# Layer 3's self-attention: rounded probabilities as low bytes of half-precision words, their base taken off by products

## The chip, the cores and the metric

The kernel runs on one core of a Trainium2 chip. The metric is the device time of one launch in microseconds (us). A profiled execution records every instruction with its start, its duration and the wait before it; its own time stands beside its span below. Engine names are those of the profile: PE is TensorE's matmul, PEld its weight load, DVE VectorE, ACT ScalarE, POOL GpSimd, SPq the queue of SyncE, from which the DMAs start.

## What is computed

Four small transformer layers follow each other on a state of 2 images x 512 tokens x 128 features, with a context of 2 x 77 x 128. The change concerns the self-attention of the fourth, layer 3, with 16 heads of 8 features. Queries, keys, probabilities and values are quantised to 8 bits there. Cut to this attention, the reference is:

```python
def _fq(x, delta, zp, n_bits):
    xi = _round_ste(x / delta) + zp
    xq = jnp.clip(xi, 0.0, 2.0 ** n_bits - 1.0)
    return (xq - zp) * delta
q, k, v = heads of h1 @ wq, h1 @ wk, h1 @ wv          # h1 = layer norm of x
sim  = einsum('bhid,bhjd->bhij', _fq(q, dq, 128.0, 8), _fq(k, dk, 128.0, 8)) * SCALE
attn = softmax(sim)
out  = einsum('bhij,bhjd->bhid', _fq(attn, dw, 0.0, 8), _fq(v, dv, 128.0, 8))
x = out @ wo + bo + x
```

So each probability becomes an integer from 0 to 255, each value an integer from -128 to 127, and their products are summed over 512 keys for every head and query.

## The kernel before, in words

Each engine has its own program (`block.sync`, `block.gpsimd`, `block.tensor`, `block.scalar`, `block.vector`), and semaphores tie them together. The self-attention of layer 3 is a pipeline over PAIRS = 64 pairs of heads: 2 images (b) x 4 values of v x 4 blocks of 128 queries (qb) x 2 pairs (`pair_of`). The 128 partitions of a tile are 4 bands of 32, and a pair is two neighbouring bands, j = 0 and 1; head 4 * band + v lies in a band at features 8 v to 8 v + 7. For pair n:

- PE (`int_scores`, L1339) makes the scores of both bands, 2 x 128 queries x 512 keys, in PSUM banks 2 (n % 3) and the next. It waits until the exponentials of pair n-3 have left these banks.
- DVE (`maxima`, L2197) reduces them to a negated maximum per query and head. POOL (`shift`, L565) multiplies it by the scale. ACT (L1644) takes two exponentials of 512 columns with their sums into a ring of six tiles (`e_ring`, parts of `e_buf` and `t_buf`); each sum comes out of its accumulator by a short instruction of its own.
- Once for two pairs, DVE (`recips`, L2203 and L2204) multiplies four sums by the step and takes the reciprocals.
- POOL (`rounded`, L574) multiplies the exponentials by the reciprocal and writes them as int16, which rounds, into `t_rows`, two instructions of 128 x 512. This is done for pair n-3 (ROUND_BEHIND) after the shift of pair n.
- SP (L411) starts one DMA transpose per pair, 128 x 1024 two-byte words, from `t_rows` to `t_turned`, rings of TURNING = 5.
- DVE (`keys`, L2210) clamps the transposed integers at 255 and converts them to bf16 in `t_keys`, a ring of four, for pair n-7 (KEYS_BEHIND) behind the maxima of pair n.
- PE (`int_outputs`, L1359) multiplies them by the values in `v_band` for pair n-8 (VALUES_BEHIND) behind the scores of pair n: 8 products of 128 columns, one per block of keys and band, each with a weight of 128 x 32 into its band of bank 7. The values of one head stand in its 8 of 32 columns and the others are zero, so that all heads of a band add up in one bank. Four products with a zero weight (L1353) open the bank for each image.

The order of work on each engine is that of the program text: for every n PE does scores of n, outputs of n-8; DVE maxima of n, `prepare(n)` (values, second half of queries and keys, key masks, for n up to 12), reciprocals, keys of n-7; POOL shift of n, rounding of n-3; ACT the exponentials of n. At fixed n other work is woven in: at 40 the output projection of image 0 (L785 on PE, 8 products; `add_to_x` on DVE), statistics and normalisation at 41 to 47, at 44 a reciprocal square root on POOL (L482, L484), at 48 and 50 a transposition and the cross queries on PE, at 52 to 54 their conversion on DVE, at 60 to 64 dummy products on PE (`keep_warm`, L641), and from 66 the first scores of the cross-attention (`first`, L1067). POOL's program ahead of the stage ends with the normalisations of layer 2 and 3 (`rstds_of`, L482 and L484; `add_bias`, L496).

```python
for n in range(PAIRS + KEYS_BEHIND):        # DVE
    if n < PAIRS: maxima(n)
    prepare(n)
    m = n - ROUND_BEHIND
    if 0 <= m < PAIRS and m % 2 == 0: recips(m // 2)
    if n >= KEYS_BEHIND: keys(n - KEYS_BEHIND)
```

Of the kernel before, what the change touches and what calls it, by code (L numbers as in the profile page):

```python
# [9 lines left out]
I16 = mybir.dt.int16  # L10
ALU = mybir.AluOpType
# [3 lines left out]
P = 128  # L15
# [79 lines left out]
TURNING = 5  # L95
# [25 lines left out]
MAX_AT = 320  # L121

# [24 lines left out]
def build(nc, ins, out, stop=99):  # L147
    ctx = ExitStack()
    with ctx:
# [29 lines left out]
        def S(name):  # L179
# [101 lines left out]
        v_band = q_stack[:, 6 * NT:10 * NT].rearrange("p (t b h c) -> p t b h c", b=B, h=H, c=BAND)  # L281
        t_rows = [k_stack[:, i * NT:(i + 1) * NT].bitcast(I16).rearrange("p (j n) -> p j n", j=2) for i in range(TURNING)]
        t_turned = [k_stack[:, i * NT:(i + 1) * NT].bitcast(I16) for i in range(TURNING, 2 * TURNING)]
        t_keys = [k_stack[:, i * NT:(i + 1) * NT] for i in range(2 * TURNING, 2 * TURNING + 4)]
# [6 lines left out]
            for places in (((q_stack[:, 10 * NT:], 0), (q_stack[:, 10 * NT:], 1)),  # L291
                           ((q_stack[:, 10 * NT:], 2), (q_stack[:, 10 * NT:], 3), (k_stack[:, (2 * TURNING + 4) * NT:], 0)),
                           ((k_stack, 0), (k_stack, 1), (k_stack, 2))))
        flat_rows, flat_turned = ([a.bitcast(I16) for a in t] for t in (flat_rows, flat_turned))

# [5 lines left out]
        v_one = sb("v_one", [P, QB, B, H, VW])  # L301
        e_ring = [e_buf[:, i // 2, i % 2 * NT:(i % 2 + 1) * NT].rearrange("p (j n) -> p j n", j=2) for i in range(4)]
# [75 lines left out]
        def _(sp):  # L378
# [26 lines left out]
            if stop >= 3:  # L405
                for n in range(PAIRS):
                    done, value = turned(n)
                    sp.wait_ge(S("ints.rounded"), 2 * (n + 1))
                    if n >= TURNING:
                        sp.wait_ge(S("ints.pt"), n - TURNING + 1)  # L410
                    sp.dma_start_transpose(t_turned[n % TURNING].rearrange("p (c q) -> p c q", q=P),  # L411
                                           t_rows[n % TURNING].rearrange("p j n -> p (j n)")).then_inc(done, 16)
                for i in range(T):
                    done, value = turned(PAIRS + i)
                    sp.wait_ge(S("cross.rounded"), i + 1)
                    if i >= len(flat_turned):
                        sp.wait_ge(S("cross.keys"), i - len(flat_turned) + 1)
                    sp.dma_start_transpose(flat_turned[i % len(flat_turned)].rearrange("p (c q) -> p c q", q=P),
                                           flat_rows[i % len(flat_rows)]).then_inc(done, 16)
# [9 lines left out]
        def _(pool):  # L429
# [130 lines left out]
            def shift_pairs():  # L560

                def shift(n):
                    c = 2 * (n % 8)
                    pool.wait_ge(S("ints.nm"), n + 1)
                    pool.tensor_scalar(stats[:, 1, c:c + 2], stats[:, 0, c:c + 2], sders[:, 8:9], None, ALU.mult  # L565
                                       ).then_inc(S("ints.m"), 1)

                def rounded(n):
                    pool.wait_ge(S("ints.recip"), n // 2 + 1)
                    if n >= TURNING:  # L570
                        pool.wait_ge(*turned(n - TURNING))
                    for j in range(2):
                        c = 2 * (n % 8) + j
                        pool.tensor_scalar(t_rows[n % TURNING][:, j, :], e_ring[n % len(e_ring)][:, j, :],  # L574
                                          stats[:, 2, c:c + 1], 0.0, ALU.mult, ALU.add).then_inc(S("ints.rounded"), 1)

                for n in range(PAIRS + ROUND_BEHIND):
                    if n < PAIRS:
                        shift(n)
                    if n >= ROUND_BEHIND:  # L580
                        rounded(n - ROUND_BEHIND)
                    if n == RSTD_AT:
                        rstds_of("L3.ln2", 0)
# [14 lines left out]
            if stop >= 2:  # L598
# [9 lines left out]
                for h in range(B):  # L608
                    rstds_of("L2.ln3", h)
                    add_bias("L2.ff", "L2.ln3.xh", h, h + 1)  # L610
            if stop >= 3:
# [14 lines left out]
        def _(pe):  # L626
# [697 lines left out]
            if stop >= 3:  # L1324
# [18 lines left out]
                def int_outputs(n):  # L1343
                    pair, b, v, qb = pair_of(n)
                    pe.wait_ge(S("ints.pt"), n + 1)
# [5 lines left out]
                    if n % (PAIRS // B) == 0:  # L1351
                        for band in range(BANDS):
                            pe.matmul(ps[BAND * band:BAND * (band + 1), 7, :], no_weight[:, :], half(k_int, b),  # L1353
                                      start=True, stop=False)
                    for kb in range(QB):
                        for j in range(2):
# [3 lines left out]
                                           v_band[:, kb, b, V * band + v, :], t_keys[n % len(t_keys)][:, c:c + P],  # L1360
# [306 lines left out]
        def _(dve):  # L1667
# [462 lines left out]
            if stop >= 3:  # L2130
# [29 lines left out]
                def values(k):  # L2160
                    dve.wait_ge(S("L3.v.base"), 1)
                    for v in range(V):
                        ins = dve.tensor_scalar(
                            v_band[:, :, k, :, :].rearrange("p t (j v) c -> p t j v c", v=V)[:, :, :, v, DH * v:DH * (v + 1)],
                            gel[:, k, :].rearrange("p (t j v d) -> p t j v d", t=QB, j=BANDS, v=V)[:, :, :, v, :],
                            MAGIC, None, ALU.subtract)
                    ins.then_inc(S("L3.values"), 1)
# [38 lines left out]
                def keys(n):  # L2206
                    dve.wait_ge(*turned(n))
                    if n >= len(t_keys):
                        dve.wait_ge(S("ints.pv"), n - len(t_keys) + 1)
                    dve.tensor_scalar(t_keys[n % len(t_keys)], t_turned[n % TURNING], QMAX, None, ALU.min  # L2210
                                      ).then_inc(S("ints.pt"), 1)

                cross_maxima, cross_recips, rest = cross()
                for n in range(PAIRS + KEYS_BEHIND):
# [6 lines left out]
                    if n >= KEYS_BEHIND:  # L2221
                        keys(n - KEYS_BEHIND)
# [66 lines left out]
```

## Time and profile before

| | before |
|---|---|
| median of 3 runs | 520.34 us (519.62 to 522.51) |
| the profiled execution, its own time | 520.02 us |
| its span, first to last instruction | 518.2 us |
| mean granted clock of TensorE, share of 2.4 GHz | 0.864 |
| PE busy, share of the span | 414.1 us, 80% |
| DVE | 354.9 us, 68% |
| ACT | 254.6 us, 49% |
| POOL | 241.1 us, 47% |

The self-attention of layer 3 lies between about 306 and 444 us of the span. The busy shares are over the whole program; what an engine does in this stage is read from windows. Neighbouring instructions of one engine overlap a little in the records, so a group's busy time is somewhat above the time from its first start to the next group's start. The weight loads run beside the products.

### The profile page before, as it was taken

To read this page: it belongs to the slowest core of one execution; us is meant where nothing else is said; L and a number is where in the kernel's file an instruction comes from. 1 tells how busy PE (TensorE), PEld (TensorE's weight loads), DVE (VectorE), ACT (ScalarE), POOL (GpSimd) and SP (SyncE) were. 2 spreads that over 40 slices of the span, in tenths; PEclk is the share of its full clock that TensorE was granted. 3 is DMA by queue.
4 is the path that set the end of the run, shared out by engine and by line. 5 is a ranking of instruction groups with operands and counts; after the bars stand their busy time and mean duration, and the time that the engine had idled before them with its cause. 6 is when DMAs were issued, how large, how long until landed. Compare 5 with 4: busy or idle time off the path is not lost.

```text
span 518.2 us, 8441 instructions
## 1 busy us (share of the span) xinstructions
PE 414.1 (80%) x2920; PEld 206.7 (40%) x2932; DVE 354.9 (68%) x802; ACT 254.6 (49%) x513; POOL 241.1 (47%) x378
## 2 busy tenths in 40 slices
PE   5999878898888999998998753666655668977797
PEld 3647544544335334333345530222232223433536
DVE  1756764559999012266873489999989898689552
ACT  2224434232002667634354338899977784457441
POOL 5052234565000443525010326999978897236420
PEclk9899999999999999999999995555565655689999
DMA  9500000000000000000000004798876669113301
GB/s 254 180 1 3 3 2 0 1 0 1 2 1 0 1 1 2 1 1 1 0 2 1 1 1 58 147 151 152 145 123 122 116 133 159 28 25 76 77 0 42
DMA packets 88976, 26.11 MB, mean 50 GB/s; under 512 B 81061, under 2 KB 88167, under 8 KB 88935
## 3 DMA queue, kind: packets, MB, share of 16 engines
q1 hardware_dynamic: 88935, 25.58, 25.5%
q8 instruction: 24, 0.39, 0.3%
q14 instruction: 17, 0.14, 0.1%
HBM read 5.61 MB, written 0.52 MB: 12 GB/s over the span
## 4 chain that ended last, share of the span: by engine, by line
PE 40%; DVE 29%; POOL 20%; issue 6%; DMA 2%; ACT 2%; POOLq 0%; DVEq 0%; ACTq 0%
POOL k_stack L574 12%; DVE k_stack L2117 9%; PE ps L849 5%; PE ps L864 4%; POOL stats L565 3%; PE ps L751 3%; DVE stats L2197 3%; PE ps L644 3%; DVE xh L1688 3%; PE ps L761 2%; DVE st L1679 2%; PE ps L641 2%; POOL rstd L484 2%; PE ps L825 2%; PE ps L927 1%
## 5 line engine op out<-in xcount | busy, mean ns | idle before, releaser
L2197 DVE TENSOR_REDUCE stats<-ps 128x2 f32<-128x1024 f32 x64 | 77.7, 1214 | 2.4 <-PE ps L1339 2.1
L1644 ACT ACTIVATE e_buf<-ps,stats,sders 128x512 f32<-128x512 f32 x88 | 67.7, 774 | 18.4 <-POOL stats L565 18.4
L1359 PE MATMUL ps<-k_stack,q_stack 128*32 128x128 bf16 x512 | 37.7, 302 | 36.9 <-DVE k_stack L2210 36.9
L574 POOL TENSOR_SCALAR k_stack<-e_buf,stats 128x512 int16<-128x512 f32 x88 | 62.7, 723 | 2.1 <-DVE stats L2204 1.5
L1490 ACT ACTIVATE e_buf<-ps 128x1024 f32<-128x1024 f32 (+3 forms) x44 | 28.2, 710 | 58.3 <-PE ps L849 58.3
L431 POOL TENSOR_SCALAR_AFFINE_SELECT e_buf<-e_buf 128x256 f32<-128x256 f32 x44 | 17.7, 411 | 66.0 <-ACT e_buf L1490 65.4
L1359 PEld LDWEIGHTS ps<-k_stack,q_stack 128*32 128x32 bf16 x512 | 21.5, 127 | 67.1 <-DVE k_stack L2210 64.5
L2117 DVE TENSOR_REDUCE k_stack<-ps 128x4 f32<-128x1024 f32 (+3 forms) x32 | 44.8, 1484 | 2.5 <-PE ps L808 2.5
L1339 PE MATMUL ps<-q_stack 32*128 32x512 bf16 x128 | 36.8, 575 | 12.2 <-ACT e_buf L1644 8.7
L482 POOL TENSOR_SCALAR rstd<-mv 128x4 f32<-128x4 f32 x18 | 4.4, 242 | 85.4 <-DVE mv L1682 85.4
L849 PE MATMUL ps<-k_stack,q_stack 32*128 32x512 f32 (+3 forms) x256 | 34.7, 478 | 0.6 <-ACT e_buf L1490 0.4
L1644 ACT ACTIVATE t_buf<-ps,stats,sders 128x512 f32<-128x512 f32 x40 | 30.8, 774 | 6.4 <-POOL stats L565 6.2
L805 PE MATMUL ps<-q_stack,qk 32*128 32x256 f32 (+3 forms) x256 | 26.3, 479 | 8.1 <-DVE k_stack L2117 8.1
L565 POOL TENSOR_SCALAR stats<-stats,sders 128x2 f32<-128x2 f32 x64 | 23.5, 367 | 17.7 <-DVE stats L2197 17.4
L1814 DVE COPY v_rows<-ps 128x512 f32<-128x512 f32 x16 | 11.0, 688 | 29.8 <-PE ps L864 22.9
L1411 ACT ACTIVATE xT<-ps,cols 128x512 f32<-128x512 f32 x16 | 12.4, 778 | 36.9 <-PE ps L631 36.9
L1688 DVE TENSOR_SCALAR xh<-x,mv,rstd 128x128 f32<-128x128 f32 x68 | 20.3, 362 | 12.8 <-POOL rstd L484 12.7
L1724 DVE TENSOR_TENSOR x<-ps,x 128x512 f32<-128x512 f32 x14 | 9.7, 691 | 28.2 <-PE ps L785 14.7
L2210 DVE TENSOR_SCALAR k_stack<-k_stack 128x1024 bf16<-128x1024 int16 x64 | 28.1, 442 | 1.0 <-DMA k_stack<-k_stack 1.0
L574 POOL TENSOR_SCALAR k_stack<-t_buf,stats 128x512 int16<-128x512 f32 x40 | 28.2, 716 | 0.6 <-DVE stats L2204 0.2
L751 PE MATMUL ps<-l_w,e_buf 128*128 128x128 f32 x192 | 22.6, 277 | 2.4 <-ACT e_buf L1471 2.4
L751 PEld LDWEIGHTS ps<-l_w,e_buf 128*128 128x128 f32 x192 | 21.9, 192 | 5.5 <-ACT e_buf L1471 3.4
(281 smaller groups left out, 897.4 us busy)
## 6 DMA issues: line engine op xcount, KB each, us to landing
wsq<-in_squares SPq DMA_DIRECT2D x3, 384.0 KB, 5.2
k_stack<-k_stack SPq DMA_TRANSPOSE x64, 3.1
spread<-in_spread SPq DMA_DIRECT2D x1, 896.0 KB, 6.7
x<-in_x SPq DMA_DIRECT2D x1, 512.0 KB, 4.4
l_w<-in_L_xattn_W_ff SPq DMA_DIRECT2D x2, 256.0 KB, 7.1
l_w<-in_L_xattn_fc_w SPq DMA_DIRECT2D x2, 256.0 KB, 7.7
l_w<-in_L_xattn_ff_w SPq DMA_DIRECT2D x1, 512.0 KB, 8.7
out<-x SPq DMA_DIRECT2D x2, 256.0 KB, 2.3
```

The lines of the kernel that those rows point to most:

```text
L565: pool.tensor_scalar(stats[:, 1, c:c + 2], stats[:, 0, c:c + 2], sders[:, 8:9], None, ALU.mult).then_inc(S("ints.m"), 1)
L574: pool.tensor_scalar(t_rows[n % TURNING][:, j, :], e_ring[n % len(e_ring)][:, j, :], stats[:, 2, c:c + 1], 0.0, ALU.mult, ALU.add).then_in ...
L751: mm = pe.matmul(o, tile(hid[:, c, :], k * QB + t), w2[:, c, :], start=(c == 0), stop=(c == FC - 1))
L849: mm = pe.matmul(ps[:, 2 * slot + j % 2, 0:N - kb * P], k1[r, v, b * N + kb * P:b * N + (kb + 1) * P], q_shift[r, b, v, kb * P:N], start=T ...
L1339: mm = pe.matmul(ps[:, 2 * (n % 3) + j % 2, :], tile(q_int, b * QB + qb)[r, :], k_band[r, v, b * N:(b + 1) * N], start=True, stop=True)
L1359: mm = pe.matmul(ps[BAND * band:BAND * (band + 1), 7, qb * P:(qb + 1) * P], v_band[:, kb, b, V * band + v, :], t_keys[n % len(t_keys)][:, ...
L1490: act.activation(e_ring[n % len(e_ring)][:, :, 0:N - kb * P], ps[:, 2 * (n % 3):2 * (n % 3) + 2, 0:N - kb * P], ACT.Exp).then_inc(S("heads ...
L1644: act.activation(e_ring[n % len(e_ring)][:, j, :], ps[:, 2 * (n % 3) + j, :], ACT.Exp, bias=stats[:, 1, c:c + 1], scale=sders[:, 8:9], acc ...
L1688: ins = dve.tensor_scalar(xh[:, t, :], x[:, t, :], mv[:, t, 0:1], rstd[:, t:t + 1], ALU.subtract, ALU.mult)
L2117: dve.tensor_reduce(nm, ps[:, bank:bank + 4, c:c + (qb + 1) * P], AX, ALU.max, negate=True).then_inc(S("heads.max"), 1)
L2197: dve.tensor_reduce(stats[:, 0, c:c + 2], ps[:, 2 * (n % 3):2 * (n % 3) + 2, :], AX, ALU.max, negate=True).then_inc(S("ints.nm"), 1)
L2210: dve.tensor_scalar(t_keys[n % len(t_keys)], t_turned[n % TURNING], QMAX, None, ALU.min).then_inc(S("ints.pt"), 1)
```

## The change

The rounding on POOL writes its result as uint8 into the low byte of each 16-bit word of `t_rows`, with the clamp at 255 in the same instruction (min in place of + 0). The high bytes are set once, before the stage, to 0x64, so that each word read as a half-precision number is 1024 + the integer. The DMA transposes the words as before, and PE reads them from `t_turned` without a conversion; DVE's `keys` is gone, and the rings `t_rows` and `t_turned` have seven places. `v_band` becomes half precision, and its heads are ordered by v and then by band, so that the weights of two neighbouring bands lie side by side. The surplus of 1024 times the sum of the values is taken off by products with a tile of -1024 (`minus_base`): for key block 0 by one product of 512 columns per image with all 128 values (`v_first`) as the weight, which also opens the bank in place of the four zero products, and for key blocks 1 to 3 by one product of 128 columns per pair and block, whose weight is the 64 columns of both bands. SP waits for PE's outputs (`ints.pv`) of pair n-7 where it waited for the clamp of pair n-5. POOL gets two memsets ahead of the normalisations of layer 3, and DVE one small conversion per image for `v_first`. The diff, cut to its core:

```diff
-TURNING = 5
+TURNING = 7
+BYTE_BASE = 1024.0
+TWO_HIGH = float(np.array([0x64006400], np.uint32).view(np.float32)[0])
...
-        v_band = q_stack[:, 6 * NT:10 * NT].rearrange("p (t b h c) -> p t b h c", b=B, h=H, c=BAND)
+        v_band = q_stack[:, 6 * NT:10 * NT].bitcast(F16).rearrange("p (t b h c) -> p t b h c", b=B, h=H, c=BAND)
         t_rows = [k_stack[:, i * NT:(i + 1) * NT].bitcast(I16).rearrange("p (j n) -> p j n", j=2) for i in range(TURNING)]
         t_turned = [k_stack[:, i * NT:(i + 1) * NT].bitcast(I16) for i in range(TURNING, 2 * TURNING)]
-        t_keys = [k_stack[:, i * NT:(i + 1) * NT] for i in range(2 * TURNING, 2 * TURNING + 4)]
+        t_keys = [a.bitcast(F16) for a in t_turned]
...
+        minus_base = k_stack[:, 15 * NT + 512:16 * NT].bitcast(F16)
+
+        def low_bytes(a):
+            return a.bitcast(U8).rearrange("p (n two) -> p n two", two=2)[:, :, 0]
...
+        v_first = v_one[:, :, :, :, :].rearrange("p t b h w -> p (t b h w)").bitcast(F16)[:, 0:B * D].rearrange(
+            "p (b d) -> p b d", b=B)
...
                     sp.wait_ge(S("ints.rounded"), 2 * (n + 1))
                     if n >= TURNING:
-                        sp.wait_ge(S("ints.pt"), n - TURNING + 1)
+                        sp.wait_ge(S("ints.pv"), n - TURNING + 1)
...
                     for j in range(2):
                         c = 2 * (n % 8) + j
-                        pool.tensor_scalar(t_rows[n % TURNING][:, j, :], e_ring[n % len(e_ring)][:, j, :],
-                                          stats[:, 2, c:c + 1], 0.0, ALU.mult, ALU.add).then_inc(S("ints.rounded"), 1)
+                        pool.tensor_scalar(low_bytes(t_rows[n % TURNING][:, j, :]), e_ring[n % len(e_ring)][:, j, :],
+                                          stats[:, 2, c:c + 1], QMAX, ALU.mult, ALU.min).then_inc(S("ints.rounded"), 1)
 
+                pool.wait_ge(S("L3.high"), 1)
                 for n in range(PAIRS + ROUND_BEHIND):
...
+            if stop >= 3:
+                pool.wait_ge(S("heads.e"), count("L2.ca", "e") + 2 * B * V)
+                pool.wait_ge(S("heads.maxT"), count("L2.ca", "maxT") + B * V)
+                pool.memset(minus_base[:, :], -BYTE_BASE).then_inc(S("L3.minus"), 1)
+                pool.memset(k_stack[:, 0:TURNING * NT].bitcast(F32), TWO_HIGH).then_inc(S("L3.high"), 1)
...
                 def int_outputs(n):
                     pair, b, v, qb = pair_of(n)
-                    pe.wait_ge(S("ints.pt"), n + 1)
+                    pe.wait_ge(*turned(n))
                     pe.wait_ge(S("L3.values"), b + 1)
...
                     if n % (PAIRS // B) == 0:
-                        for band in range(BANDS):
-                            pe.matmul(ps[BAND * band:BAND * (band + 1), 7, :], no_weight[:, :], half(k_int, b),
-                                      start=True, stop=False)
+                        pe.wait_ge(S("L3.minus"), 1)
+                        pe.matmul(ps[:, 7, :], v_first[:, b, :], minus_base[:, :], start=True, stop=False)
                     for kb in range(QB):
+                        if kb:
+                            h = BANDS * v + 2 * pair
+                            two = v_band[:, kb, b, h:h + 2, :].rearrange("p h c -> p (h c)")
+                            pe.matmul(ps[2 * BAND * pair:2 * BAND * (pair + 1), 7, qb * P:(qb + 1) * P], two,
+                                      minus_base[:, 0:P], start=False, stop=False)
                         for j in range(2):
                             band = 2 * pair + j
                             c = (j * QB + kb) * P
                             mm = pe.matmul(ps[BAND * band:BAND * (band + 1), 7, qb * P:(qb + 1) * P],
-                                           v_band[:, kb, b, V * band + v, :], t_keys[n % len(t_keys)][:, c:c + P],
+                                           v_band[:, kb, b, BANDS * v + band, :], t_keys[n % len(t_keys)][:, c:c + P],
                                            start=False, stop=(v == V - 1 and qb == QB - 1 and kb == QB - 1))
...
+                    ins = dve.tensor_scalar(v_first[:, k, :], gel[:, k, 0:P], MAGIC, None, ALU.subtract)
                     ins.then_inc(S("L3.values"), 1)
...
-                def keys(n):
-                    dve.wait_ge(*turned(n))
-                    if n >= len(t_keys):
-                        dve.wait_ge(S("ints.pv"), n - len(t_keys) + 1)
-                    dve.tensor_scalar(t_keys[n % len(t_keys)], t_turned[n % TURNING], QMAX, None, ALU.min
-                                      ).then_inc(S("ints.pt"), 1)
...
-                    if n >= KEYS_BEHIND:
-                        keys(n - KEYS_BEHIND)
```

## Rows read from the trace of the kernel before

**Rows 1.** Windows: stretch, length, busy us (count) per engine, PEclk, DMA share

```profile
332.00:381.50 49.50, 31.75 (x280) 12.53 (x282) 49.02 (x86) 44.95 (x112) 48.70 (x84) 0.50 0.86 148
381.50:415.00 33.50, 20.07 (x164) 8.96 (x158) 28.99 (x58) 23.80 (x59) 26.16 (x45) 0.60 0.66 115
415.00:431.50 16.50, 12.21 (x93) 4.46 (x94) 16.33 (x31) 14.44 (x36) 16.15 (x28) 0.50 0.77 137
```

**Rows 2.** Chain of waits, 335 to 383 us, its shares by line

```profile
by line: POOL k_stack L574 71.0%; POOL stats L565 20.1%; issue 9.7%; POOLq L571 0.0%
```

**Rows 3.** Order of time, 359 to 364 us: start, duration, instruction

```profile
360.15 0.46 DVE L2210 TENSOR_SCALAR k_stack<-k_stack 128x1024 bf16<-128x1024 int16 x1
...
360.33 0.43 POOL L565 TENSOR_SCALAR stats<-stats,sders 128x2 f32<-128x2 f32 x1
...
360.66 0.61 PE L1359 MATMUL ps<-k_stack,q_stack 128*32 128x128 bf16 x8 [0.35 <-DVE k_stack L2210]
360.73 1.35 POOL L574 TENSOR_SCALAR k_stack<-e_buf,stats 128x512 int16<-128x512 f32 x2
360.79 0.78 ACT L1644 ACTIVATE t_buf<-ps,stats,sders 128x512 f32<-128x512 f32 x1 [0.31 <-POOL stats L565]
...
361.20 0.61 PE L1339 MATMUL ps<-q_stack 32*128 32x512 bf16 x2
...
361.65 0.44 DVE L2203 TENSOR_TENSOR stats<-stats,scalars 128x4 f32<-128x4 f32 x1
...
362.38 0.78 ACT L1644 ACTIVATE t_buf<-ps,stats,sders 128x512 f32<-128x512 f32 x1
362.40 1.46 POOL L574 TENSOR_SCALAR k_stack<-e_buf,stats 128x512 int16<-128x512 f32 x2
...
363.86 0.43 POOL L565 TENSOR_SCALAR stats<-stats,sders 128x2 f32<-128x2 f32 x1
```

**Rows 4.** Order of time, POOL, 397 to 399 us

```profile
397.12 0.29 POOL L565 TENSOR_SCALAR stats<-stats,sders 128x2 f32<-128x2 f32 x1
...
398.71 0.29 POOL L565 TENSOR_SCALAR stats<-stats,sders 128x2 f32<-128x2 f32 x1
```

**Rows 5.** Order of time: POOL's shifts of six pairs; PE's first cross scores

```profile
322.15 0.32 POOL L565 TENSOR_SCALAR stats<-stats,sders 128x2 f32<-128x2 f32 x1
...
331.89 0.57 POOL L565 TENSOR_SCALAR stats<-stats,sders 128x2 f32<-128x2 f32 x1
...
381.54 0.43 POOL L565 TENSOR_SCALAR stats<-stats,sders 128x2 f32<-128x2 f32 x1
...
385.81 0.29 POOL L565 TENSOR_SCALAR stats<-stats,sders 128x2 f32<-128x2 f32 x1 [2.52 <-DVE stats L2197]
...
415.13 0.65 POOL L565 TENSOR_SCALAR stats<-stats,sders 128x2 f32<-128x2 f32 x1 [0.21 <-DVE stats L2197]
...
431.26 0.28 POOL L565 TENSOR_SCALAR stats<-stats,sders 128x2 f32<-128x2 f32 x1
...
434.77 2.23 PE L1067 MATMUL ps<-km,q_stack 128*128 128x462 bf16 x6
```

**Rows 6.** Groups by line and shape, 350 to 383 us, DVE

```profile
L2210 DVE TENSOR_SCALAR k_stack<-k_stack 128x1024 bf16<-128x1024 int16 x19 | 8.3, 436 | 0.0
```

**Rows 7.** Groups by line and shape, POOL, whole span

```profile
L455 POOL MEMSET k_stack<- 128x4096 f32 x1 | 3.5, 3513 | 0.0
...
L457 POOL MEMSET v_one<- 128x128 f32 x1 | 0.3, 321 | 0.0
...
L434 POOL MEMSET ident<- 128x128 f32 x1 | 0.2, 205 | 0.3 <-POOLq L2267 0.3
```

**Rows 8.** DMA issues of the page: count, us to landing

```profile
k_stack<-k_stack SPq DMA_TRANSPOSE x64, 3.1
```

**Rows 9.** Order of time, POOL's last wait before layer 3

```profile
298.79 0.23 POOL L482 TENSOR_SCALAR rstd<-mv 128x4 f32<-128x4 f32 x1 [6.18 <-DVE mv L1682]
```

**Rows 10.** Order of time, DVE, values of image 0

```profile
309.69 0.62 DVE L2163 TENSOR_SCALAR q_stack<-gel 128x128 bf16<-128x128 f32 x4
```

More of the change, by code:

```diff
@@ L10 @@
 I16 = mybir.dt.int16
+U8 = mybir.dt.uint8
 ALU = mybir.AluOpType
@@ L291, in build @@
             for places in (((q_stack[:, 10 * NT:], 0), (q_stack[:, 10 * NT:], 1)),
-                           ((q_stack[:, 10 * NT:], 2), (q_stack[:, 10 * NT:], 3), (k_stack[:, (2 * TURNING + 4) * NT:], 0)),
+                           ((q_stack[:, 10 * NT:], 2), (q_stack[:, 10 * NT:], 3), (k_stack[:, 14 * NT:], 0)),
                            ((k_stack, 0), (k_stack, 1), (k_stack, 2))))
         flat_rows, flat_turned = ([a.bitcast(I16) for a in t] for t in (flat_rows, flat_turned))
+        minus_base = k_stack[:, 15 * NT + 512:16 * NT].bitcast(F16)
+        def low_bytes(a):
+            return a.bitcast(U8).rearrange("p (n two) -> p n two", two=2)[:, :, 0]
         km = q_stack[:, 0:8 * NT].bitcast(F32).rearrange("p (v n) -> p v n", v=V)
@@ L2163, in values @@
                         ins = dve.tensor_scalar(
-                            v_band[:, :, k, :, :].rearrange("p t (j v) c -> p t j v c", v=V)[:, :, :, v, DH * v:DH * (v + 1)],
+                            v_band[:, :, k, :, :].rearrange("p t (v j) c -> p t j v c", v=V)[:, :, :, v, DH * v:DH * (v + 1)],
                             gel[:, k, :].rearrange("p (t j v d) -> p t j v d", t=QB, j=BANDS, v=V)[:, :, :, v, :],
                             MAGIC, None, ALU.subtract)
+                    ins = dve.tensor_scalar(v_first[:, k, :], gel[:, k, 0:P], MAGIC, None, ALU.subtract)
                     ins.then_inc(S("L3.values"), 1)
```

## The prediction

> **What bounds the kernel now.** No engine is full over the whole run, as the table above has it, so the stage that the change touches has to be read by itself. The windows come first [rows 1]. From 332 to 381.5 us POOL is busy 48.70 of 49.50 us and DVE 49.02, while ACT has 44.95 and PE 31.75 at a granted clock of 0.50, which is the 1.2 GHz level. Two engines look full. The chain of waits tells which one sets the pace: from 335 to 383 us it is POOL's rounding (71.0%) and its shift (20.1%), and DVE is not in it [rows 2]. The order of time shows why both look full [rows 3]. POOL's shifts two pairs apart start at 360.33 and 363.86, so a pair takes 3.53 / 2 = 1.77 us. DVE has no gap in that time, but part of it is waiting: its tensor_tensor on four elements starts at 361.65 and takes 0.44 us, until 362.09, just when POOL's roundings end (360.73 + 1.35). POOL loses as well: the shift at 360.33, which starts under DVE's clamp of 360.15, takes 0.43 us where one without a clamp beside it takes 0.29 [rows 4], and the two roundings at 362.40 take 1.46 against the 1.35 of those at 360.73. So the two engines hinder each other, and each clamp that goes helps both. Where no clamp lies beside them, POOL takes 1.59 us for a pair, 397.12 to 398.71 [rows 4].
>
> The whole stage can be counted by POOL's shifts, one for each pair [rows 5]: pair 7 at 322.15, pair 12 at 331.89, pair 40 at 381.54, pair 54 at 415.13, pair 63 at 431.26. Pair 41 starts at 385.81. That is 1.95, 1.77, 2.40 and 1.79 us a pair. The 2.40 come from the projection, the normalisation and the cross queries that are woven in there and stop the loop, and it shows in the windows too: POOL 26.16 busy of 33.50 [rows 1].
>
> **The parts of the change.**
>
> *The clamps go* (64 of DVE, 0.436 us each [rows 6]; I count 0.35, since neighbours on DVE overlap by some 0.1). DVE falls from 1.77 to about 1.42 us a pair, and is no longer beside the bound. POOL falls from 1.77 towards 1.59. ACT is the next: from the first exponential of one pair to the first of the next it takes 360.79 to 362.38 = 1.59 us [rows 3]. Two engines with the same 1.59 that wait for each other will not run without a gap; I take 1.62. The bounds are 1.59 and the old 1.77.
>
> *Low bytes and min in the rounding* (128 POOL instructions). No row shows a byte output with a step of two, nor a min on POOL. The nearest instruction is the same one with int16 out, 0.67 us a piece. From below: no extra, since f32 in and one result per element stay; a gain has no reason. From above: a strided write in the trace, the memset of 128 single elements 36 bytes apart, takes 0.321 us where 128 adjacent ones take 0.205 [rows 7], which is 0.116 per 128, or 0.46 us for 512 elements. I take 0, because two bytes is much nearer to adjacent than 36, and keep the 0.46 as a rival. The Trainium skill (GPSIMD Engine Reference, Performance pitfalls for Q7 kernels) puts a price of half as much again on reads whose step is over 8 bytes, and says nothing of writes; by it a step of 2 costs nothing, and the sum would be the one I give, while by the memset's row it would be some 55 us more.
>
> *Base products* (per pair 3 more products of 128 columns, 64 wide, over both bands; per image one product of 512 columns in place of four). Today the eight products of a pair take 0.54 us to the next start (360.66 to 361.20), four steps of two bands side by side at 128 columns per 1.2 GHz = 0.107 us, and 0.11 around them [rows 3]. The three new ones cannot lie beside the others, as they cover both bands: 3 x 0.107 = 0.32 us. PE then has 0.54 (scores) + 0.54 + 0.32 = 1.40 of 1.62 us. Hidden, but with little cover; a change of tile width could cost more, up to the 0.11 that surrounds a group now, six times a pair: 2.06 us. I take 0 for it, as the change from one band to the next costs nothing visible.
>
> *Transposes.* Same 64, same bytes, from SP's queue; SP now waits for PE's outputs of pair n-7 instead of the clamp of pair n-5, which is long past. They land in 3.1 us [rows 8] and the DMA share is 0.86 at 1.77 us a pair [rows 1], so full use would be at 1.52 us a pair. PE now reads what they land, and behind this wait stand the next scores, for which DVE's maxima wait. PE's outputs of pair n-8 come about two paces and 0.9 us after the rounding ended: 4.1 us against 3.1. Cost 0, at most the pace of 1.52.
>
> *POOL's two memsets* (3584 words and 512 half words) before the stage. At 3.51 us for 4096 elements [rows 7] they take 3.1 + 0.5 us. They fall into POOL's idle time of 6.18 us before 298.79 [rows 9]: 0, and over 2 us of cover is left.
>
> *Two more conversions for v_first* on DVE, beside the first maxima, where DVE is the bound; four conversions of 128 elements take 0.62 us today [rows 10]: 2 x 0.15 = +0.3 us.
>
> **The sum.** Up to pair 7: +0.3. Pairs 7 to 12: DVE had masks besides (9.74 us); without clamps 5 x 1.63 = 8.15, -1.6. Pairs 12 to 40: 49.65 becomes 28 x 1.62 = 45.4, -4.3. Pairs 40 to 54, 33.6 us: four long steps, of 13.9 us together (the longest is 381.54 to 385.81 [rows 5]), are waits round the whole loop and stay; the other ten take 1.97 each, since DVE has additions and statistics between its maxima, and fall to about 1.67: -3.0. Pairs 54 to 63: 9 x 1.62, and 0.5 more because the dummy products there come on top of a fuller PE: 16.1 becomes 15.1, -1.0. Tail: the first cross scores come 3.5 us after the last shift now (431.26 to 434.77 [rows 5]); without the clamp at the end of that wait 2.6, -0.9, but four outputs between them and the projection are 0.32 longer, +1.3. Together -9.2 us. The profiled execution took 520.0 us with a span of 518.2, so 510.8; the median of the runs is 0.3 higher: **511 us**.
>
> **The rivals.**
>
> *POOL's byte writes cost more* (slower). For it: no row shows such a write, and the strided memset is dearer. Against it: the memset's step is 18 times as long. The pace rises by twice the extra for a rounding. It gives all back when a rounding takes over 0.75 us instead of 0.67, since (1.77 - 1.62) / 2 = 0.08. At 0.46 more the pace is 2.54 us, 60 pairs x 0.92 = 55 us over the forecast: 566 us. At 0.80 us a rounding it is about 527. Chance 0.15.
>
> *PE becomes the bound.* At six changes of width for 0.06 us each PE has 1.76 us a pair and the pace stays: about 519 us; at 0.11 each 2.06 us, about 535. Against it: a fuller PE may be granted 2.4 GHz at times, as between 381.5 and 415 us, where the mean is 0.60 [rows 1]. The Trainium skill (TensorE: Matmul & The Clock Gate, The mechanism) lets a weight load overlap a running product only in another row group; all of these use all rows, so by it three loads more lie open, about 0.1 us each, and PE would have 1.7 us. The trace speaks against it: eight loads today fit in the 0.54 us. Chance 0.11, a quarter of it slower.
>
> *The loop of ACT, PE, DVE and POOL does not close in 1.62* (or the transposes come late), and the pace only falls to 1.70: 28 pairs give 2.0, the rest about half, 515 us. For it: ACT has gaps of 0.31 us behind POOL's shift already, one of them before 360.79 [rows 3]. Chance 0.13.
>
> *The forecast*, 0.61.
>
> **How the numbers follow.** Half a percent, about what a measurement can tell from no change here, is 2.6 us: faster is below 517.7. Forecast and slow loop are faster, 0.74; PE as the bound is mostly the same, 0.08 and with leftovers 0.09; byte writes and the dear end of PE slower, 0.17. The low end, 503, is the pace of 1.59 everywhere, the long gaps shortened by half and a faster PE in the tail; the high end, 519, takes in the slow loop and PE at the old pace. The byte writes stay outside.
>
> **What would show it.** POOL's roundings in pairs of 1.35 us and shifts of 0.29, without the longer ones; shift starts 1.60 to 1.65 us apart between pairs 12 and 40; DVE idle before its maxima; PE's output groups 0.86 us to the next start and PE's share near nine tenths. Roundings of 0.75 us or more, output groups over 1.1 us, or PE waiting for the transposes would each prove a step wrong.

## The result, and the profile after

The changed kernel takes 668.89 us (667.12 to 671.74, 4 runs) against 521.12 us of the kernel before in the same session (519.62 to 522.51, 4 runs): a ratio of 1.284, 95% interval 1.281 to 1.288. It is 148 us slower where 9 us less were forecast, and outside the range.

Of the page of the changed kernel, the span, the busy shares, and the costliest groups with their mean ns behind the busy time:

```profile
span 665.5 us, 8692 instructions
...
PE 483.5 (73%) x3105; PEld 237.1 (36%) x3118; DVE 339.1 (51%) x740; ACT 255.7 (38%) x513; POOL 402.7 (61%) x380
...
L584 POOL TENSOR_SCALAR k_stack<-e_buf,stats 128x512 uint8<-128x512 f32 x88 | 175.8, 2023 | 0.6 <-DVE stats L2225 0.5
...
L1379 PE MATMUL ps<-k_stack,q_stack 128*32 128x128 f16 x512 | 74.3, 288 | 7.9 <-DMA k_stack<-k_stack 7.4
...
L1374 PE MATMUL ps<-k_stack,q_stack 128*64 128x128 f16 x192 | 60.7, 316 | 0.0
```

and the rounding in the page of the kernel before:

```profile
L574 POOL TENSOR_SCALAR k_stack<-e_buf,stats 128x512 int16<-128x512 f32 x88 | 62.7, 723 | 2.1 <-DVE stats L2204 1.5
```

A rounding (now L584) takes 2023 ns where it took 723, and PE has 192 new products (L1374) beside its 512. The window that answers to [rows 1]:

```profile
332.00:500.00 168.00, 90.26 (x520) 38.73 (x520) 61.01 (x95) 65.57 (x161) 167.74 (x121) 0.50 0.32 62
```

POOL is busy 167.74 of 168 us, DVE and ACT a good third each, PE 90 at the 1.2 GHz level. The chain of waits from 335 to 560 us, as in [rows 2]:

```profile
by line: POOL k_stack L584 85.4%; issue 8.4%; POOL stats L575 7.0%; POOL rstd L492 0.1%; POOL rstd L494 0.1%; POOLq L581 0.0%
```

So POOL sets the pace even more than before, and by the rounding alone. The order of time around one pair, all engines, as in [rows 3]:

```profile
399.69 4.01 POOL L584 TENSOR_SCALAR k_stack<-e_buf,stats 128x512 uint8<-128x512 f32 x2
399.79 0.78 ACT L1664 ACTIVATE t_buf<-ps,stats,sders 128x512 f32<-128x512 f32 x1 [2.59 <-POOL stats L575]
...
401.56 0.61 PE L1355 MATMUL ps<-q_stack 32*128 32x512 bf16 x2 [2.00 <-ACT t_buf L1664]
...
402.09 0.29 PE L1379 MATMUL ps<-k_stack,q_stack 128*32 128x128 f16 x2
...
402.31 0.32 PE L1374 MATMUL ps<-k_stack,q_stack 128*64 128x128 f16 x1
...
402.56 0.29 PE L1379 MATMUL ps<-k_stack,q_stack 128*32 128x128 f16 x2
...
403.66 0.31 POOL L575 TENSOR_SCALAR stats<-stats,sders 128x2 f32<-128x2 f32 x1
...
407.88 0.31 POOL L575 TENSOR_SCALAR stats<-stats,sders 128x2 f32<-128x2 f32 x1
```

Two things stand in it. POOL's shifts, at 403.66 and 407.88, are 4.22 us apart, of which the two roundings take 3.97 (399.69 to 403.66); ACT waits 2.59 us for each shift and PE 2.00 for ACT. And PE's outputs of a pair, from 402.09 on, go in steps of 0.47 us: two products side by side to the next start 0.22, the base product 0.25. Four steps without the first base are 1.62 us, where the forecast had 0.86. In this kernel that is hidden under POOL.

The pace accounts for the time. The last shift starts at 569.93 us where it started at 431.26 [rows 5], 138.7 later. Some 9 us more stand behind it, 95.5 us to the end of the span against 86.9: POOL still has eight roundings of the last pairs to do there, at 2 us each.

The memsets did not fall where the prediction put them:

```profile
288.35 3.09 POOL L626 MEMSET k_stack<- 128x3584 f32 x1
291.40 0.23 POOL L492 TENSOR_SCALAR rstd<-mv 128x4 f32<-128x4 f32 x1
...
298.64 0.23 POOL L492 TENSOR_SCALAR rstd<-mv 128x4 f32<-128x4 f32 x1 [3.38 <-DVE mv L1702]
```

They follow the bias at 286.68 at once and push back the reciprocal square root for image 0, not the wait before image 1. DVE's normalisation waits 4.27 us for it:

```profile
292.79 1.11 DVE L1708 TENSOR_SCALAR xh<-x,mv,rstd 128x128 f32<-128x128 f32 x4 [4.27 <-POOL rstd L494]
```

It costs nothing all the same: the next reciprocal square root is at 298.64, against 298.79 before [rows 9], since DVE waits for PE's work for layer 2 in between, and only waits less: its next addition starts at 296.54 after 2.63 us of waiting, against 296.69 after 5.42 before. The stage's first shift is at 307.42 and was at 307.50.

### The profile page after: what moved, and what is told of

It is laid out like the page before. It is cut to its first block, busy times and chain, and to the rows that moved or that the text cites. A ratio compares the mean times of both kernels' runs of the same rounds, so it can differ in the third digit from the quotient of the medians.

```text
span 665.5 us, 8692 instructions
## 1 busy us (share of the span) xinstructions
PE 483.5 (73%) x3105; PEld 237.1 (36%) x3118; DVE 339.1 (51%) x740; ACT 255.7 (38%) x513; POOL 402.7 (61%) x380
## 4 chain that ended last, share of the span: by engine, by line
POOL 41%; PE 30%; DVE 20%; issue 6%; ACT 2%; DMA 2%; DVEq 0%; ACTq 0%; POOLq 0%
POOL k_stack L584 35%; DVE k_stack L2137 7%; PE ps L865 4%; PE ps L880 3%; POOL stats L575 3%; PE ps L767 2%; DVE xh L1708 2%; PE ps L660 2%; PE ps L777 2%; DVE st L1699 1%; PE ps L657 1%; PE ps L841 1%; PE ps L943 1%; POOL rstd L494 1%; PE ps L801 1%
## 5 line engine op out<-in xcount | busy, mean ns | idle before, releaser
L584 POOL TENSOR_SCALAR k_stack<-e_buf,stats 128x512 uint8<-128x512 f32 x88 | 175.8, 2023 | 0.6 <-DVE stats L2225 0.5
L1379 PE MATMUL ps<-k_stack,q_stack 128*32 128x128 f16 x512 | 74.3, 288 | 7.9 <-DMA k_stack<-k_stack 7.4
L584 POOL TENSOR_SCALAR k_stack<-t_buf,stats 128x512 uint8<-128x512 f32 x40 | 79.9, 2022 | 0.0
L1374 PE MATMUL ps<-k_stack,q_stack 128*64 128x128 f16 x192 | 60.7, 316 | 0.0
L1355 PEld LDWEIGHTS ps<-q_stack 32*128 32x128 bf16 x128 | 8.1, 99 | 126.5 <-issue 126.0
L1379 PEld LDWEIGHTS ps<-k_stack,q_stack 128*32 128x32 f16 x512 | 26.4, 101 | 58.7 <-issue 25.9
L2224 DVE TENSOR_TENSOR stats<-stats,scalars 128x4 f32<-128x4 f32 x32 | 10.6, 331 | 64.4 <-ACT e_buf L1664 43.2
L1374 PEld LDWEIGHTS ps<-k_stack,q_stack 128*64 128x64 f16 x192 | 24.7, 128 | 22.5
L575 POOL TENSOR_SCALAR stats<-stats,sders 128x2 f32<-128x2 f32 x64 | 20.9, 327 | 10.3 <-DVE stats L2218 10.3
```

What stands on the lines that cost most here:

```text
L584: pool.tensor_scalar(low_bytes(t_rows[n % TURNING][:, j, :]), e_ring[n % len(e_ring)][:, j, :], stats[:, 2, c:c + 1], QMAX, ALU.mult, ALU. ...
L1355: mm = pe.matmul(ps[:, 2 * (n % 3) + j % 2, :], tile(q_int, b * QB + qb)[r, :], k_band[r, v, b * N:(b + 1) * N], start=True, stop=True)
L1374: pe.matmul(ps[2 * BAND * pair:2 * BAND * (pair + 1), 7, qb * P:(qb + 1) * P], two, minus_base[:, 0:P], start=False, stop=False)
L1379: mm = pe.matmul(ps[BAND * band:BAND * (band + 1), 7, qb * P:(qb + 1) * P], v_band[:, kb, b, BANDS * v + band, :], t_keys[n % len(t_keys)] ...
```

## The experiments

Two questions were open: what makes the rounding dear (a byte as the result, its step, or the min), and whether the rest of the forecast holds once that is gone. From bytes_add on, the kernels leave the clamp at 255 out, except clamp_back; forms and ops only add instructions at the end of the kernel before.

**The forms of the instruction by themselves.** Behind POOL's last work, in the kernel before:

```diff
+                for dt, step in ((I16, 1), (I16, 2), (U8, 1), (U8, 2), (U8, 4), (BF16, 1), (F32, 1)):
...
+                    for name, s2, op in (("add", 0.0, ALU.add), ("min", QMAX, ALU.min)):
...
+                        pool.tensor_scalar(d, src, ident[:, 0:1], s2, ALU.mult, op).then_inc(S("micro"), 1)
```

> The kernel before, with 42 more POOL instructions behind its last work: 128x512 f32 read from one tile and written to another, as int16, int16 with a step of two words, uint8 with steps of 1, 2 and 4 bytes, bf16 and f32, each once with mult and add and once with mult and min, three times over. Nothing of the computation is left out; its time means nothing, since these stand at its end. Theory byte store: in the changed kernel a rounding takes 2.0 us because its result is one byte wide, whatever the step; then uint8 takes 2.0 us at every step and with either operation, and all other types 0.7. Rival step: uint8 at step 1 takes 0.7 and only the stepped ones 2.0, int16 at step 2 too. Rival min: all forms with min take 2.0 and all with add 0.7.

Measured, first round, in the order of the text (add, then min): int16 at step 1 0.69 and 2.02, at step 2 0.83 and 2.15; uint8 at step 1 0.69 and 1.99, at step 2 0.70 and 2.00, at step 4 0.83 and 2.14; bf16 0.69 and 1.99; f32 0.69 and 1.99. In the order of time (start, duration, instruction), int16 at step 1 with add and with min, uint8 at step 2 with add and with min:

```profile
518.84 0.69 POOL L633 TENSOR_SCALAR sin_t<-cos_t,ident 128x512 int16<-128x512 f32 x1 [16.24 <-DVE x L1738]
...
519.63 2.02 POOL L633 TENSOR_SCALAR sin_t<-cos_t,ident 128x512 int16<-128x512 f32 x1
...
527.78 0.70 POOL L633 TENSOR_SCALAR sin_t<-cos_t,ident 128x512 uint8<-128x512 f32 x1
...
528.57 2.00 POOL L633 TENSOR_SCALAR sin_t<-cos_t,ident 128x512 uint8<-128x512 f32 x1
```

The first theory, that a byte as the result is dear, falls, and so does the step: the min costs 1.3 us on 512 columns whatever is written, and a byte in every second place costs what a word costs. Steps of four bytes cost 0.14.

**Bytes and min in the kernel before**, all else left, but that the high bytes are set to zero once:

```diff
-                        pool.tensor_scalar(t_rows[n % TURNING][:, j, :], e_ring[n % len(e_ring)][:, j, :],
-                                          stats[:, 2, c:c + 1], 0.0, ALU.mult, ALU.add).then_inc(S("ints.rounded"), 1)
+                        pool.tensor_scalar(low_bytes(t_rows[n % TURNING][:, j, :]), e_ring[n % len(e_ring)][:, j, :],
+                                          stats[:, 2, c:c + 1], QMAX, ALU.mult, ALU.min).then_inc(S("ints.rounded"), 1)
```

> The kernel before, with the rounding alone changed: mult and min into the low bytes of words whose high bytes POOL has set to zero once; the clamp on DVE, the bf16 copies and the zero products stay as before, so nothing of the computation is left out. Theory byte store: a rounding takes 2.02 us as in the changed kernel, a pair 2 x 1.97 + 0.3 = 4.2 us on POOL, and the time is that of the changed kernel, 665 to 675 us. Rival, that the products or the wait on the transposes share the loss: the time stays clearly below, under 640 us.

Measured 673.46 us, ratio 1.292 (1.286 to 1.298). The window of the same stretch:

```profile
332.00:500.00 168.00, 47.92 (x400) 20.22 (x402) 86.99 (x133) 64.11 (x157) 167.74 (x120) 0.51 0.32 61
```

This one instruction carries the whole loss. The changed kernel has 1.284 (1.281 to 1.288), and the two intervals just overlap, so nothing that the rest of the change costs or gains can be told from noise as long as POOL is that slow.

**The changed kernel with add in place of min:**

```diff
-                                          stats[:, 2, c:c + 1], QMAX, ALU.mult, ALU.min).then_inc(S("ints.rounded"), 1)
+                                          stats[:, 2, c:c + 1], 0.0, ALU.mult, ALU.add).then_inc(S("ints.rounded"), 1)
```

> The changed kernel with one operation undone: the rounding into low bytes is mult and add 0, as before the change, in place of mult and min 255. The clamp is left out. Theory min: the table of forms has uint8 with a step of two at 0.69 us with add and 2.0 with min, so the whole loss through POOL goes, and PE's eleven products are left as in words: 540 to 550 us. Rival bytes: written beside the transposes and DVE, single bytes cost more than in the table: over 560 us.

Measured 544.85 us, ratio 1.044 (1.034 to 1.055). POOL's order of time:

```profile
356.14 0.29 POOL L575 TENSOR_SCALAR stats<-stats,sders 128x2 f32<-128x2 f32 x1 [0.52 <-DVE stats L2218]
356.40 1.36 POOL L584 TENSOR_SCALAR k_stack<-e_buf,stats 128x512 uint8<-128x512 f32 x2
358.30 0.29 POOL L575 TENSOR_SCALAR stats<-stats,sders 128x2 f32<-128x2 f32 x1 [0.54 <-DVE stats L2218]
```

The roundings into bytes are back at 1.36 us for two, with the transposes and DVE beside them, and the shifts now wait 0.52 us for DVE. So a second bound was hidden under POOL: 2.16 us a pair.

**The same in whole words:**

```diff
+                        pool.tensor_scalar(t_rows[n % TURNING][:, j, :], e_ring[n % len(e_ring)][:, j, :],
+                                          stats[:, 2, c:c + 1], float(0x6400), ALU.mult, ALU.add).then_inc(S("ints.rounded"), 1)
```

> The changed kernel, with POOL's rounding writing whole 16-bit words again: mult and add 25600 (0x6400) into int16, which gives the same words without the memset of the high bytes. The clamp at 255 is left out. The rest of the change stays. Theory PE next: the records of the changed kernel show 1.62 us for the eleven products of a pair instead of the 0.86 forecast, with 0.54 for the scores 2.16 us a pair at 1.2 GHz, so PE sets the pace: 1.77 -> 2.16 over some 51 pairs is +20 us, 535 to 542 us. Rival forecast: a fuller PE is granted 2.4 GHz most of the time, or its groups overlap more than they seem, and POOL's 1.6 us a pair holds: 508 to 514 us.

Measured 543.24 us (541.21 to 548.42, three runs; a fourth, whose profile is shown, took 549.85), ratio 1.044 (1.037 to 1.052), at the top of the range expected and above it. The window, the chain of waits from 335 to 375 us, and PE's scores, first outputs and next scores in the order of time:

```profile
332.00:410.00 78.00, 77.55 (x462) 33.13 (x461) 48.83 (x82) 56.20 (x138) 57.43 (x106) 0.50 0.64 119
```

```profile
by line: PE ps L1377 41.3%; PE ps L1372 34.5%; PE ps L1353 24.3%
```

```profile
371.10 0.61 PE L1353 MATMUL ps<-q_stack 32*128 32x512 bf16 x2
...
371.63 0.29 PE L1377 MATMUL ps<-k_stack,q_stack 128*32 128x128 f16 x2
...
373.26 0.61 PE L1353 MATMUL ps<-q_stack 32*128 32x512 bf16 x2
```

Scores are 2.16 us apart, 0.54 for themselves and 1.62 for the outputs, PE is busy 77.55 of 78 us, and the chain is PE's alone. The same window of bytes_add, whose profiled execution took 548.51 us, has PE busy 77.55 us at 0.50 too. The clock stays at 0.50, the 1.2 GHz level, all through: the records show a full PE, and no rise. The hope that a fuller PE pulls its clock up falls here.

The theory priced only the pace, and that part came as expected: in the profile, the time from first to last shift is 18.8 us longer than in the kernel before. The rest of the 29.8 us between the two spans stands outside: 2.0 ahead of the first shift and 9.0 behind the last.

**No base products in the pairs:** four of 512 columns at the start of each image instead, with all values as weights.

```diff
-                        pe.matmul(ps[:, 7, :], v_first[:, b, :], minus_base[:, :], start=True, stop=False)
+                        for kb in range(QB):
+                            pe.matmul(ps[:, 7, :], v_first[:, b, kb, :], minus_base[:, :], start=(kb == 0), stop=False)
...
-                        if kb:
-                            h = BANDS * v + 2 * pair
...
```

> As words, but the base is taken off all four key blocks at the start of an image, by four products of 512 columns with all 128 values of a block as the weight, and no base product is left in the pairs. The clamp at 255 is left out as in words. Theory PE next: output groups are back at 0.54 us, PE at 1.1 us a pair, and POOL sets the pace at about 1.62: 508 to 513 us. Rival loop: the wait of PE on the transposes or the round through ACT, PE, DVE and POOL keeps the pace at 1.7 to 1.77: 516 to 521 us.

Measured 509.09 us (507.86 to 511.32), ratio 0.977 (0.973 to 0.981): faster than both kernels.

And with bytes instead of words, by the add 0 of bytes_add:

> As words_once, with the rounding into low bytes by mult and add 0 instead of words by mult and add 25600; the high bytes are set once. The clamp is left out of the arithmetic. Theory min: a byte costs what a word costs, the memset of the high bytes is hidden: 508 to 511 us, the same as words_once. Rival bytes: each rounding is dearer by more than 0.05 us in place and the time is over 514 us.

Measured 507.04 us (506.81 to 513.77), ratio 0.976 (0.968 to 0.985), as words_once within the intervals. Its window and its shifts of pairs 12, 40, 41, 54 and 63:

```profile
332.00:375.00 43.00, 30.45 (x262) 12.33 (x260) 39.29 (x56) 42.77 (x107) 42.75 (x80) 0.50 0.95 163
```

```profile
331.57 0.32 POOL L575 TENSOR_SCALAR stats<-stats,sders 128x2 f32<-128x2 f32 x1
...
376.62 0.29 POOL L575 TENSOR_SCALAR stats<-stats,sders 128x2 f32<-128x2 f32 x1
...
382.21 0.29 POOL L575 TENSOR_SCALAR stats<-stats,sders 128x2 f32<-128x2 f32 x1 [3.97 <-DVE stats L2214]
...
407.03 0.45 POOL L575 TENSOR_SCALAR stats<-stats,sders 128x2 f32<-128x2 f32 x1
...
421.73 0.29 POOL L575 TENSOR_SCALAR stats<-stats,sders 128x2 f32<-128x2 f32 x1
```

From pair 12 to 40 a pair takes 45.05 / 28 = 1.61 us. POOL, ACT and the DMAs are all near full here (42.75 and 42.77 of 43 us, share 0.95). The chain of waits from 335 to 375 us is still POOL's, 74.9% rounding and 16.8% shift.

**Why the eleven products take 1.62 us.** Two ways to keep base products in the pairs. In words_narrow a base product is made for each band, in words_grouped the loop over the base products stands ahead of the loop over the others; the first:

```diff
+                            for band in (2 * pair, 2 * pair + 1):
+                                pe.matmul(ps[BAND * band:BAND * (band + 1), 7, qb * P:(qb + 1) * P],
+                                          v_band[:, kb, b, BANDS * v + band, :], minus_base[:, 0:P], start=False, stop=False)
```

> As words, but each base product of 64 columns is made as two of 32, one for each band, with the same weights as the products that follow. The clamp is left out. Theory width: the extra 0.76 us of a pair on PE over the forecast comes from the six changes between 64 and 32 columns, about 0.12 each; with one width there is none, three steps more of two bands side by side give 0.54 + 0.32 = 0.86 us, PE 1.40 us a pair, POOL the pace again: 508 to 515 us. Rival load: every product in a band that was just used waits for its weight, whatever its width; the group stays at 1.3 us or more and the time over 525.

Measured 509.14 us, ratio 0.976 (0.969 to 0.983). PE's order of time:

```profile
359.64 0.61 PE L1353 MATMUL ps<-q_stack 32*128 32x512 bf16 x2
360.18 0.29 PE L1376 MATMUL ps<-k_stack,q_stack 128*32 128x128 f16 x2
360.26 0.31 PE L1371 MATMUL ps<-k_stack,q_stack 128*32 128x128 f16 x2
360.37 0.31 PE L1376 MATMUL ps<-k_stack,q_stack 128*32 128x128 f16 x2
...
361.12 0.61 PE L1353 MATMUL ps<-q_stack 32*128 32x512 bf16 x2
```

Here fourteen products take 361.12 - 360.18 = 0.94 us with the wait for the next scores; within the group two lie side by side and the next two follow after 0.11. Three products more than the change had, and 0.7 us less.

> As words, but the three base products of a pair stand together ahead of its eight others, so the width changes twice a pair and not six times. The clamp is left out. Theory width: 0.54 + 0.32 + one more change of 0.12 to 0.25 = 0.98 to 1.1 us for the group, PE 1.5 to 1.65 us a pair, beside POOL's 1.6: 509 to 520 us. Rival load: three wide products in a row each wait for their weight, 0.25 each: 1.3 us, PE 1.85 us, 524 to 530 us.

Measured 509.12 us, ratio 0.976 (0.969 to 0.983):

```profile
359.72 0.61 PE L1353 MATMUL ps<-q_stack 32*128 32x512 bf16 x2
360.26 0.53 PE L1371 MATMUL ps<-k_stack,q_stack 128*64 128x128 f16 x3
360.47 0.31 PE L1371 MATMUL ps<-k_stack,q_stack 128*64 128x128 f16 x1
360.72 0.61 PE L1377 MATMUL ps<-k_stack,q_stack 128*32 128x128 f16 x8
361.26 0.61 PE L1353 MATMUL ps<-q_stack 32*128 32x512 bf16 x2
```

The second row is the third of the three wide products by itself. They start at 360.26, 360.37 and 360.47, 0.107 us apart like any others, and the first narrow one follows 0.24 after the last wide one; the eight narrow ones take 0.54 to the next scores, as ever. That is 1.00 us for the same eleven products. So the wide product costs what the forecast took for it, and the alternation is dear: six changes between 64 and 32 columns in place of one cost 1.62 - 1.00 = 0.62 us more, 0.12 each. In the changed kernel a change to the wide product costs 0.22 - 0.11 = 0.11 us over a step, one back 0.25 - 0.11 = 0.14, and six of them make up the 0.76 us between 1.62 and the forecast's 0.86. The 0.11 that surrounded a group in the kernel before was such a change already, between the 32 x 128 weights of the scores and the 128 x 32 ones of the outputs.

The rival that every weight is waited for falls. But the weight loads do behave differently at a change. Of the changed kernel, the load of the first wide product, and of words_grouped, the loads of the second and third:

```profile
402.31 0.13 PEld L1374 LDWEIGHTS ps<-k_stack,q_stack 128*64 128x64 f16 x1
```

```profile
360.28 0.26 PEld L1371 LDWEIGHTS ps<-k_stack,q_stack 128*64 128x64 f16 x2
```

At a change the load starts together with its product, 402.31 for both; in a row of one width it starts ahead, 360.28 for the product at 360.37, while the first wide product (360.26) is still running. Whether this missing lead is what a change costs, or only goes with it, no run separates.

**The clamp put back on DVE**, behind words_once:

```diff
+                def keys(n):
+                    dve.wait_ge(*turned(n))
+                    a = t_turned[n % TURNING]
+                    dve.tensor_scalar(a, a, float(0x6400 + 255), None, ALU.min).then_inc(S("ints.pt"), 1)
```

> As words_once, with the clamp put back on DVE for pair n-7, on the turned words in place (128x1024 int16, min 0x64FF), and PE's products waiting for it. Nothing of the computation is left out here. Theory shared clamp: what words_once gains over the kernel before is DVE's clamp beside POOL's work; with it back DVE and POOL hinder each other again, a pair takes 1.74 to 1.77 us and the time is 517 to 521 us. Rival products: the gain is in PE reading without the bf16 copies or the longer rings, and the time stays at 508 to 513 us.

Measured 524.85 us over 10 runs, ratio 1.005 (1.003 to 1.008). POOL's order of time:

```profile
358.81 0.59 POOL L575 TENSOR_SCALAR stats<-stats,sders 128x2 f32<-128x2 f32 x1
359.15 1.45 POOL L584 TENSOR_SCALAR k_stack<-t_buf,stats 128x512 int16<-128x512 f32 x2
360.59 0.43 POOL L575 TENSOR_SCALAR stats<-stats,sders 128x2 f32<-128x2 f32 x1
361.00 1.36 POOL L584 TENSOR_SCALAR k_stack<-t_buf,stats 128x512 int16<-128x512 f32 x2
362.33 0.59 POOL L575 TENSOR_SCALAR stats<-stats,sders 128x2 f32<-128x2 f32 x1
```

Shifts of 0.43 and 0.59 and roundings of 1.45 are back, two pairs take 3.52 us, and from pair 12 to 40 a pair takes 1.77 us, as in the kernel before. All that words_once gains over the kernel before is this clamp: with it back, nothing is left. The time is even some 3 us above both the range expected and the kernel before; 1.9 us of that stands ahead of the stage in the profile, whose first shift is at 309.44 against 307.50.

**Which operations are dear on POOL:**

> The kernel before, with 27 more POOL instructions behind its last work: 128x512 f32 to int16 with nine forms of one or two operations, three times over: mult and add, mult and min, mult and max, mult and subtract, mult and mult, min and mult, max and min, mult alone, min alone. Nothing of the computation is left out; its time means nothing. Theory comparison: an operation that compares costs POOL 2.0 us wherever it stands, min or max, first, second or alone, and arithmetic ones 0.7. Rival second place: min is dear only as the second operation, and min first or alone is 0.7. Rival list: mult with add is the one fast pair, and mult with subtract or mult are at 2.0 as well.

```profile
518.36 0.70 POOL L631 TENSOR_SCALAR sin_t<-cos_t,ident 128x512 int16<-128x512 f32 x1 [16.23 <-DVE x L1737]
...
523.36 2.00 POOL L631 TENSOR_SCALAR sin_t<-cos_t,ident 128x512 int16<-128x512 f32 x1
...
525.46 0.70 POOL L631 TENSOR_SCALAR sin_t<-cos_t,ident 128x512 int16<-128x512 f32 x1
...
530.45 1.58 POOL L629 TENSOR_SCALAR sin_t<-cos_t,ident 128x512 int16<-128x512 f32 x1
```

Shown are mult with add, with subtract, with mult, and mult alone. All nine, in the order of the text: mult and add 0.70, mult and min 2.02, mult and max 2.00, mult and subtract 2.00, mult and mult 0.70, min and mult 2.00, max and min 2.00, mult alone 1.58, min alone 1.56. The theory of comparisons falls with subtract, and with mult alone, which is dearer than mult with a second operation that changes nothing (the add of 0 in forms, 0.69). The rival of a short list of fast pairs stands, though mult with mult is on it too.

## Why the prediction was wrong

**The step that failed** is the second part of the change, "Low bytes and min in the rounding": "I take 0". It priced the write and passed over the operation. Its upper bound came from a strided memset and was 0.46 us; measured were 1.30 (uint8 at step 2, 2.00 against 0.70 us), all from the min. That is also why the range missed: the rival was named ("POOL's byte writes cost more") with the point from which it decides, 0.75 us a rounding, and its formula is right, twice the extra a pair: 1.62 + 2 x 1.30 = 4.22 us, as measured. But its mechanism, the write, and its size were wrong. The sentence "nor a min on POOL" stood in the text, and no bound followed from it. The row of the same instruction with add says nothing of the price with min: an instruction whose operation has not been seen on that engine has an open price.

**The base products** were the second miss, hidden in the result. The prediction took 0.32 us and kept 0.11 for each change of width as the dear end. Measured is 0.12 a change, the dear end: PE 2.16 us a pair where that end had 2.06. Without the min the change would still have been slower, by 4.4%. "I take 0 for it, as the change from one band to the next costs nothing visible" compared a change of place with a change of width; words_narrow shows that the first is free, words_grouped that the second is not. And the relief that the rival was given, a clock that rises with a fuller PE, did not come: 0.50 at 77.55 busy of 78 us. The row cited for it did not support it either, for in the window with the mean of 0.60 PE is busy 20.07 of 33.50 us, less than in the one before, 31.75 of 49.50 [rows 1]. The rule of the Trainium skill on weight loads (TensorE: Matmul & The Clock Gate, The mechanism) is not borne out: fourteen loads fit in 0.94 us in words_narrow, and in words_grouped the load at 360.28 runs beside a product on the same rows. At a change of width none runs ahead.

**The rest mostly held.** bytes_once is the change without the min and without base products in the pairs, and can be laid against the sum. Pairs 7 to 12 take 8.9 us (forecast 8.15), 12 to 40 45.05 (45.4), 40 to 54 30.4 (30.6), 54 to 63 14.7 (15.1). The profiled execution is 13.2 us under that of before, where 9.2 were forecast; the pairs from 7 on give 10.0 of it, and the stretch behind the last shift another 3.7, where the forecast had 0.4 more, or 0.9 less without the base products; pair 7 comes 0.5 later. TensorE's clock is higher there: its mean is 0.78 between 421.7 and 435 us, against 0.50 between 431.3 and 445 us in the kernel before, and whether that is the reason was not tried. The pace of 1.62 and the reason for it, DVE's clamp beside POOL, are confirmed by clamp_back. The sum of the long steps came right by luck, since two misses cancel: the first grew, 376.62 to 382.21 is 5.6 us against 4.3 before, and the third, 3.1 us before, is gone (1.6), so the four take 13.4 us for 13.9. Clamp_back has the first and the third of them the same way (5.2 and 1.6 us), so DVE's clamp is not the reason; what is, stays open. The transposes carry the pace at a share of 0.95, near the bound of 1.52 us a pair that the prediction worked out; between 335 and 375 us PE waits 1.1 us for them and 9.9 for ACT.

**The memsets** cost nothing, as forecast, but for another reason: they do delay a reciprocal square root by 2.6 us, and that one has slack.

What stays open: what it is in a change of width on PE that costs the 0.12 us; whether the clamp can be had for less than on DVE, where it takes the whole gain. The versions above that beat the kernel before leave it out; with the step of these inputs, 1/255, no probability is above 255 steps, but with another step the clamp would act. Whether the conversion to a byte bounds the result by itself was not tried. Why just mult with add and mult with mult are fast on POOL is not shown by any run.

## What to carry to other kernels

Before an operation of POOL in a pipeline is swapped for another, time the new form by itself on the chip: the time goes by the pair of operations and hardly by the type or the step of the result, and a dummy second operation can be worth having. Keep products of one width together on PE, or move what is the same for many of them out of the loop. And when one engine turns out slow, look for the next bound under it before mending only the first: here the mended rounding alone would still have lost 4.4%.

## What the runs showed of the hardware that was not expected

- POOL's tensor_scalar on 128x512 f32, one after another and each waited for: 0.70 us for mult with add or mult with mult, 1.57 for mult or min alone, 2.00 for mult with min, max or subtract, min with mult, max with min.
- Its result in uint8, int16, bf16 or f32, and a step of two bytes, make no difference; a step of four bytes adds 0.14 us.
- Products of 128x64 and 128x32 on the same bands: each change of width costs 0.12 us at 1.2 GHz (0.11 to the wide one, 0.14 back); wide ones in a row are 0.107 us apart, as narrow ones are two at a time. At a change the weight load starts with its product, in a row ahead of it.
- TensorE stayed at the 1.2 GHz level for 78 us with products in 77.55 of them; all but nine had weights of 32 or 64 columns or of 32 rows.
